# Roundings and a normalisation moved from VectorE to ScalarE in the last two attentions of a transformer stack

## The reference

```
x = x + tanh(g_xattn[2]) * L2_xattn(layernorm(x), ctx)     # 8 heads of 64, context of 64 tokens
x = x + tanh(g_ffn[2])   * L2_ffn(layernorm(x))
x = x + tanh(g_xattn[3]) * L3_xattn(layernorm(x), ctx)     # the same shapes
x = x + tanh(g_ffn[3])   * L3_ffn(layernorm(x))

def act_quant(x):                                          # in L2_ffn
    scale = 127.0 / clip(max(abs(x), axis=-1, keepdims=True), 1e-5, None)
    return clip(round(x * scale), -128.0, 127.0) / scale
h = square(relu(bitlinear(x, w_gate))) * bitlinear(x, w_up)   # 128 -> 512, ternary weights
y = bitlinear(h, w_down)                                   # bitlinear = act_quant(x) @ weight_quant(w).T
# L3_ffn: r = relu(x @ W.T), y = (r * r) @ W2.T
```

## Time and profile before

| what | us |
|---|---|
| median of 3 runs (1627.86 to 1633.79) | 1629.6 |
| the profiled execution | 1627.99 |
| its span | 1626.2 |
| the part with decoder's steps 11 to 41 | 246.08 |
| the 148.76 us behind it (second attention with the last feed-forward) | 148.76 |

### The profile page before, as it was taken

The page is one execution under the profiler, slowest core; times in us unless marked ns, Lnnn a source line. Parts: engine busy times, 40 slices in busy tenths (PEclk is TensorE's granted clock), DMA queues, the critical chain, the costliest instruction groups (busy, mean ns, idle before and its releaser), DMA issues.

```text
span 1626.2 us, 51062 instructions
## 1 busy us (share of the span) xinstructions
PE 1457.0 (90%) x18081; PEld 1101.7 (68%) x18081; DVE 1192.4 (73%) x4951; ACT 876.6 (54%) x1729; POOL 605.4 (37%) x1180
## 2 busy tenths in 40 slices
PE   6999999998999679898879779998998888899998
PEld 5888888875666345454476546666777677778886
DVE  6777777766777799999946844434889989866664
ACT  6665666554554455555303245554566666655553
POOL 4555545540000666666226411102333333334331
PEclk9999999998999587878659979997999999999999
DMA  8000000005300000000020010000000000000000
GB/s 194 2 0 0 0 0 0 0 1 117 76 0 3 12 0 0 0 0 0 1 64 0 0 34 0 0 0 2 2 2 1 0 1 2 2 2 14 6 14 21
DMA packets 41754, 23.37 MB, mean 14 GB/s; under 512 B 23325, under 2 KB 39162, under 8 KB 41530
## 3 DMA queue, kind: packets, MB, share of 16 engines
q1 hardware_dynamic: 41658, 22.07, 5.9%
HBM read 17.87 MB, written 4.19 MB: 14 GB/s over the span
## 4 chain that ended last, share of the span: by engine, by line
PE 60%; DVE 25%; issue 8%; ACT 3%; POOL 2%; DVEq 1%; DMA 0%; SPq 0%; POOLq 0%; ACTq 0%
PE ps L681 7%; PE ps L690 7%; DVE arena L1354 5%; DVE arena L1348 4%; PE ps L310 3%; PE ps L352 3%; PE ps L303 3%; PE ps L332 3%; PE ps L2058 2%; PE ps L2045 2%; PE ps L343 2%; PE ps L2132 2%; PE ps L2051 2%; PE ps L323 2%; PE ps L2101 2%
## 5 line engine op out<-in xcount | busy, mean ns | idle before, releaser
L681 PE MATMUL ps<-xnT,arena 128*128 128x512 f32 x256 | 134.8, 619 | 0.0
L574 POOL TENSOR_TENSOR ln_veps<-ln_mv,eps 128x4 f32<-128x4 f32 x40 | 10.7, 268 | 268.5 <-DVE ln_mv L568 268.5
L2557 POOL TENSOR_TENSOR arena<-arena 128x512 f32<-128x512 f32 x64 | 67.8, 1059 | 111.5 <-DVE arena L2481 111.5
L1810 DVE TENSOR_SCALAR_CACHE_REDUCE thr_hits<-thr_abs,thr_candidate 128x512 bf16<-128x512 f32 (+1 forms) x248 | 101.9, 477 | 0.0
L1354 DVE MATCH_REPLACE8 arena<-arena 128x64 f32<-128x64 f32 x512 | 101.7, 208 | 0.1
L830 DVE SCALAR_TENSOR_TENSOR x_res<-ps,arena,x_res 128x128 f32 (+1 forms) x256 | 72.0, 344 | 31.1 <-PE ps L690 28.5
L530 POOL TENSOR_TENSOR arena<-arena 128x1024 f32<-128x1024 f32 x32 | 61.4, 1918 | 54.1 <-DVE arena L484 54.1
L469 DVE TENSOR_REDUCE arena<-ps 128x16 f32<-128x1024 f32 x32 | 39.2, 1224 | 57.7 <-PE ps L323 57.7
L1348 DVE MAX8 arena<-arena 128x8 f32<-128x64 f32 x512 | 76.1, 210 | 6.6 <-POOL arena L1235 5.4
L690 PEld LDWEIGHTS ps<-arena 128*128 128x128 f32 x512 | 63.6, 191 | 25.4 <-issue 17.2
L1620 PE MATMUL ps<-ident,arena 128*64 128x128 f32 x256 | 43.1, 323 | 37.6 <-DVE arena L1406 37.6
(11 more groups left out here) (405 smaller groups left out, 4252.4 us busy)
## 6 DMA issues: line engine op xcount, KB each, us to landing
toeplitz<-ssm_toeplitz_scratch SPq DMA_DIRECT2D x2, 2048.0 KB, 18.0
ssm_toeplitz_scratch<-ssm_padded_kernel SPq DMA_DIRECT2D x1, 2048.0 KB, 12.9
out<-x_res SPq DMA_DIRECT2D x8, 256.0 KB, 2.3
arena<-ctx SPq DMA_DIRECT2D x2, 768.0 KB, 5.7
arena<-L_ffn_W SPq DMA_DIRECT2D x2, 512.0 KB
arena<-L_xattn_Wo SPq DMA_DIRECT2D x3, 256.0 KB, 8.8
arena<-L_xattn_Wq SPq DMA_DIRECT2D x1, 512.0 KB, 5.9
x_res<-x SPq DMA_DIRECT2D x1, 512.0 KB, 7.2
```

The costliest lines, as they stand in the source:

```text
L681: nc.tensor.matmul(ps[:, u % 3, :], w1[:, x, c * P:(c + 1) * P], xnT, start=True, stop=True).then_inc(h_full.sem, 1)
L1810: ins = V.tensor_scalar(self.hits[:, j, at:at + n], self.abs[:, at:at + n], self.cand[:, c:c + 1].bitcast(F32), 0.0, ALU.is_ge, ALU.add, a ...
L2557: G_.tensor_tensor(probs, probs, rc[:, s, :].unsqueeze(2).to_broadcast([P, heads, CTX]), ALU.mult).then_inc(s_prob.sem, 1)
```

## The change

1. The rounding of h (L2382) leaves VectorE. ScalarE does it, as an activation Identity with the scale of each partition and ROUND as bias, right behind its copy of head outputs.
2. The square (L2290) moves on ScalarE from behind the copy of probabilities to right behind the relu.
3. The normalising of four tiles (L2347) goes to ScalarE, behind its copy of keys, for both feed-forwards. For it GpSimd makes a bias: minus the mean times the reciprocal root, two more operations of 128x4 a round.
4. The rounding of the four tiles (L2367) goes to ScalarE, behind its copy of keys, one step after. VectorE's clip (L2371) moves to the next step, ahead of the clip of h.
5. The transpose of xn goes to PSUM bank 1 (columns 256 to 383) instead of bank 4, and no longer waits for the subtraction of the maximum.

```diff
@@ turn_xn, copy_xn @@
-        T_.transpose(ps[:, 4, 256:256 + P], xn[:, s, :], k.ident[:]).then_inc(xt_full.sem, 1)
+        T_.transpose(ps[:, 1, 256:256 + P], xn[:, s, :], k.ident[:]).then_inc(xt_full.sem, 1)
@@ pe_step @@
         if ahead(r, 1):
-            e.wait_ge(s_sub.sem, s_sub.at(t + 1))
             turn_xn(e, t + 1, o)
@@ act_step @@
             copy_heads(e, t)
+        if downs(r):
+            e.wait_ge(a_recip.sem, a_recip.at(t - F2))
+            e.wait_ge(hq_done.sem, hq_done.at(t - F2 - 1))
+            S.activation(hq[:], h[:], ACT.Identity, bias=magic[:, 0:1], scale=sh[:, 0:1]).then_inc(hr_done.sem, 1)
...
             S.activation(rl[:], ps[:, 6, :], ACT.Relu, scale=cgt[:, j:j + 1]).then_inc(r_done.sem, 1)
+            e.wait_ge(r_done.sem, r_done.at(t - F2 + 1))
+            e.wait_ge(h_done.sem, h_done.at(t - F2))
+            S.activation(r2[:], rl[:], ACT.Square).then_inc(r2_done.sem, 1)
...
-        if gates(r):
-            e.wait_ge(r_done.sem, r_done.at(t - F2 + 1))
-            e.wait_ge(h_done.sem, h_done.at(t - F2))
-            S.activation(r2[:], rl[:], ACT.Square).then_inc(r2_done.sem, 1)
         if ahead(r, 1):
             copy_queries(e, t + 1)
             copy_keys(e, t + 1)
+        if norms(r, 1):
+            e.wait_ge(n_shift.sem, n_shift.at(b))
+            if r >= F3 + 2:
+                e.wait_ge(x3_full.sem, x3_full.at(b - 9))
+            for j in range(GT):
+                last = S.activation(k.xn[:, 0, j, :], k.x[:, tile_at(t, r, j, 7), :], ACT.Identity, bias=n_bias[:, j:j + 1], scale=k.rstd[:, 0, j:j + 1])
+            last.then_inc(n_out.sem, 1)
+        if norms(r, 2) and r < LN3:
+            g = b - 2
+            e.wait_ge(q_step.sem, q_step.at(4 * g + 3))
+            for j in range(GT):
+                last = S.activation(qf[:, j, :], k.xn[:, 0, j, :], ACT.Identity, bias=magic[:, 0:1], scale=sc[:, j:j + 1])
+            last.then_inc(q_step.sem, 1)
@@ quantize, and dve_step behind the subtraction of the maximum @@
-        e.wait_ge(q_step.sem, q_step.at(n + 3))
-        for j in range(GT):
-            last = V.tensor_scalar(qf[:, j, :], k.xn[:, 0, j, :], sc[:, j:j + 1], ROUND, ALU.mult, ALU.add)
-        last.then_inc(q_step.sem, 1)
-        e.wait_ge(q_step.sem, q_step.at(n + 4))
+
+    def clip_q(e, g):
+        e.wait_ge(q_step.sem, q_step.at(4 * g + 4))
         e.wait_ge(qt_full.sem, qt_full.at(g))
         V.tensor_scalar(qb[:], qf[:], -ROUND, 127.0, ALU.add, ALU.min).then_inc(q_done.sem, 1)
...
+        if turns_q(r):
+            clip_q(e, b - 2)
         if downs(r):
             clip_h(e, t)
@@ scale_h @@
-        e.wait_ge(a_recip.sem, a_recip.at(n))
-        V.tensor_scalar(hq[:], h[:], sh[:, 0:1], ROUND, ALU.mult, ALU.add).then_inc(hr_done.sem, 1)
@@ pool_step, behind the reciprocal root of four tiles @@
+            G_.tensor_tensor(n_mean[:], k.mv[:, 0, :, 0], k.rstd[:, 0, :], ALU.mult).then_inc(n_mr.sem, 1)
...
+            G_.tensor_tensor(n_bias[:], n_zero[:], n_mean[:], ALU.subtract).then_inc(n_shift.sem, 1)
```

More of the change, by code:

```diff
@@ L1940, in decoder @@
     p_full, p_laid, y_full, x_done = sem("probsT_full", STEPS), sem("probsT_laid", STEPS), sem("y_full", STEPS), sem("x_added", STEPS)
-    n_stats, n_mv, n_ve, n_rs, n_out = (sem("group_" + n, NLN) for n in ("stats", "mv", "veps", "rstd", "normed"))
+    n_stats, n_mv, n_ve, n_rs, n_mr, n_shift, n_out = (sem("group_" + n, NLN) for n in ("stats", "mv", "veps", "rstd", "mean_scaled", "shift", "normed"))
     w2_in, w2_sum, w2_tot, w2_step, w2_tern = sem("f2_w_loaded", None), sem("f2_w_sums", 1), sem("f2_w_totals", 1), sem("f2_w_step", 7), sem("f2_w_ternary", 1)
@@ L1953, in decoder @@
     h3_full, r3_done, h3_laid = (sem("f3_" + n, IC * GROUPS) for n in ("h_full", "relu", "squared"))
-    out_done = k.sem("out_stored")
+    out_done, zeroed = k.sem("out_stored"), sem("zeroed", 1)
     cv = Carve(k.arena)
@@ L1970, in decoder @@
     am, sc, cgt, cut = (cv.f32(GT) for _ in range(4))
+    n_zero, n_mean, n_bias = (cv.f32(GT) for _ in range(3))
     qf, qb, qT = cv.f32(GT, D), cv.bf16(GT, D), cv.bf16(GT * P)
@@ L1973, in decoder @@
     hb, hT = cv.bf16(HID), cv.bf16(HID)
-    ah, sh, yc = cv.f32(1), cv.f32(1), cv.f32(1)
+    ah, sh, yc, magic = cv.f32(1), cv.f32(1), cv.f32(1), cv.f32(1)
     wf, wp, tf, tp = cv.f32(IC, D), cv.f32(HID), cv.f32(IC, D), cv.f32(HID)
@@ L2222, in copy_xn @@
         e.wait_ge(xt_full.sem, xt_full.at(t + 1))
-        S.copy(xnT[:, s * P:(s + 1) * P], ps[:, 4, 256:256 + P]).then_inc(xt_laid.sem, 1)
+        S.copy(xnT[:, s * P:(s + 1) * P], ps[:, 1, 256:256 + P]).then_inc(xt_laid.sem, 1)
     def copy_queries(e, t):
@@ L2340, in group_norm @@
             last.then_inc(n_mv.sem, 1)
[L2341 to L2345, removed]
-            for j in range(GT):
-                last = V.tensor_scalar(k.xn[:, 0, j, :], k.x[:, tile_at(t, r, j, 7), :], k.mv[:, 0, j, 0:1], k.rstd[:, 0, j:j + 1],
-                                       ALU.subtract, ALU.mult)
-            last.then_inc(n_out.sem, 1)
         if norms(r, 2) and r < LN3:
@@ L2396, in dve_weights @@
                 V.tensor_reduce(sums[:, i:i + 1], wraw[:, i, :], AX.X, ALU.add, apply_absolute_value=True)
+            V.memset(magic[:], ROUND)
             V.tensor_copy(identb[:], k.ident[:]).then_inc(w2_sum.sem, 1)
@@ L2481, in dve_step @@
             V.reciprocal(rc[:, s, :], sm[:, s, :]).then_inc(s_rec.sem, 1)
-        if norms(r, 1) or norms(r, 2):
+        if norms(r, 2):
             group_norm(e, t, r, b)
@@ L2543, in pool_step @@
             G_.tensor_tensor(k.rstd[:, 0, :], k.veps[:, 0, :], k.half[:], ALU.pow).then_inc(n_rs.sem, 1)
+            e.wait_ge(n_rs.sem, n_rs.at(b))
+            if r > LN2:
+                e.wait_ge(n_out.sem, n_out.at(b - 1))
+            e.nop(nofuse=True)
+            G_.tensor_tensor(n_mean[:], k.mv[:, 0, :, 0], k.rstd[:, 0, :], ALU.mult).then_inc(n_mr.sem, 1)
+            e.wait_ge(n_mr.sem, n_mr.at(b))
+            e.nop(nofuse=True)
+            if r == LN2:
+                e.wait_ge(zeroed.sem, zeroed.at(1))
+            G_.tensor_tensor(n_bias[:], n_zero[:], n_mean[:], ALU.subtract).then_inc(n_shift.sem, 1)
         if ahead(r, 2):
@@ L2560, in pool @@
         e.wait_ge(before.sem, before.end)
+        G_.memset(n_zero[:], 0.0).then_inc(zeroed.sem, 1)
         for t in range(2):
```

## The result

| | before | changed |
|---|---|---|
| median of 6 runs, us | 1631.46 (1627.86 to 1633.92) | 1614.21 (1611.26 to 1616.83) |
| ratio to before | | 0.9898 (0.9881 to 0.9915) |
| span of the profiled run, us | 1626.2 | 1614.3 |

The kernel is 1.0% faster, 17 us; the forecast was 1609 in 1594 to 1620. The spans differ by only 11.9. Up to the first subtraction of the decoder, in code that the change doesn't touch, the changed profile took 1115.38 and that of before 1110.67 us.

What follows compares the result with a forecast made beforehand. It took a circle of VectorE and ScalarE, with TensorE waiting, to bound the fused stretch. Gains of 19.9 + 1.0 + 0.4 less 0.6 made 20.7 us, from 1627.99 to 1607.3; with 1.6 for the median, 1609, range 1594 to 1620.

Steps and rivals of the forecast that it cites:

- VectorE's relief: Fused stretch: VectorE loses 4.6 of its 28.28 us a round and no longer sets the round.
- ScalarE's prices: Moved work on ScalarE: rounding of h 0.83 us, small activations 0.53; its round goes from 20.84 to some 27.
- The stalls on top of the floor: Five TensorE delays a round, 0.6, 0.5, 0.55, 0.4 and 0.15 us, added to 26.6 to give 28.8.
- The projection behind the two batches: Output projection held behind ScalarE's normalising (0.5 us) and rounding of four tiles (0.55) in each round.
- Transposes of h: TensorE's transposes of h come late: 0.4 us in the fourth step, 0.15 in the first.
- Keys: Keys wait for the copy of transposed h, delayed by the earlier square: 0.15 us a step, 0.6 a round.
- The multiplier: Fused stretch, steps 11 to 41: 2.57 us gained a round, times 7.75 rounds, 19.9 us.
- last stretch: The 148.76 us behind the fused stretch: 0.2 us gained a round from moving the normalising, five rounds, 1.0 us.
- my own case: The main forecast, with a round of 28.8 us and a time of 1600 to 1619; chance 0.68.
- TensorE alone is left: Rival: small activations cheap and ScalarE's queue has slack, round 26.6 to 27.2 us, time about 1594; chance 0.17.
- the work only changes place: Rival: each ScalarE batch holds TensorE its whole 1.6 us, round 30.95, time about 1626; chance 0.09.
- ScalarE as the slower engine: Rival: small activations at 0.9 us each make a round 32.8 us, time 1640; chance 0.06.

Runs made afterwards that it cites:

- turn_only: The kernel before with only the transpose of xn in bank 1 and no wait for the subtraction; ratio to before 0.9983.
- h_only: The kernel before with only the rounding of h moved to ScalarE; ratio to before 0.9902.
- own_bank: The changed kernel with transposed h and tiles in otherwise unused halves of banks 4 and 3, so keys need not wait; ratio to before 0.9831, median 1604.64 us.
- norm_back: The changed kernel with the normalising of four tiles back on VectorE, without GpSimd's two operations; ratio to before 0.9895.
- norm_only: The kernel before with only the normalising of four tiles on ScalarE, with GpSimd's operations for it; ratio to before 0.9984.
- wait_back: The changed kernel with the transpose of xn back in bank 4, waiting for the subtraction; ratio to before 0.9888.
- h_back: The changed kernel with the rounding of h back on VectorE; ratio to before 0.9946.
- round_back: The changed kernel with the rounding of four tiles back on VectorE, its clip still one step later; ratio to before 0.9910.
- own_square_norm: The changed kernel with separate banks for transposed h and tiles, the square behind the copy of probabilities, normalising on VectorE; ratio to before 0.9837.

## Why the prediction was right, and where it was off

**The range and the sign** held: 1614.2 in 1594 to 1620. The gain was 17 us instead of 20.7, a fifth less.

**The bound before** was read rightly as a circle of VectorE and ScalarE on which TensorE waits. turn_only shows that the wait at the subtraction was a sign of it and no cause.

**VectorE's relief.** The sum took 4.6 us of VectorE's work as one thing ("It no longer sets the round"). The runs part it: of the three, the rounding of h alone gives 1.55 us a round and 13 of the 16 us; the normalising 0 to 0.3 a round; the rounding of four tiles 0.3, in the company of the rest. What was missing in my reading is where each stands. The rounding of h is on the circle in all four steps. The relief was also smaller than 4.6: VectorE went from 28.28 to 24.90, 3.4. The four roundings of h took 1.6 off (28.28 to 26.68 in h_only), since the next instruction starts before they end; I had taken their whole length, 1.9.

**ScalarE's prices** were right: 0.83 forecast and 0.814 measured for the rounding of h, 0.53 and 0.485 for the small ones, "some 27" and 26.86 for the round.

**The stalls on top of the floor** are what was mis-sized. Forecast 28.8 a round, measured 29.20. The projection behind the two batches: 1.05 forecast, 1.2 measured. Transposes of h: 0.55 forecast (0.4 in the fourth step, 0.15 in the first); the row reads 1.4 in all four, but the kernel before has 1.1 of the same wait within what I took as the floor, so 0.3 came on top:

```profile
PEld ps L2154 <- DVE x_res L2470: 1.1, 4, 0.3
```

Keys: "I take 0.15 a step (bounds 0 and 0.25), 0.6 in a round", measured 1.7. That is the term that failed. It left out that the copy of the four tiles stands ahead of the keys too, in the step where they are 0.66 late. It took the square at 0.55 of the queue, as if it overlapped the relu; but it reads what the relu writes and starts when that has ended (0.73 behind its start, the copy of before 0.58), so the copy of transposed h starts 1.27 us behind the relu instead of 0.58, 0.69 later. And it took off a lateness of TensorE that did not come: in the first three steps of the round its queries begin 0.52 to 0.61 us behind the relu, 0.57 before. own_bank measures what the keys' wait is worth when removed: 1.1 us a round, half a microsecond more than forecast, and that is about what the forecast missed. The three waits added to 26.6 are 29.8, more than the 29.20: they are waits of weight loads, and ahead of the keys' matmuls the idle time is only 0.9.

**The multiplier.** 2.17 us a round by 7.75 is 16.8; the stretch gave 15.95, of which 1.3 is the clock. The other rounds at full clock gave 1.84 to 2.17, and at the end of the stretch it was lost: step 40 took 9.23 us against 8.49 before. norm_back has 8.47 there, so what costs is ScalarE's batch of the normalising ahead of that step.

**Around it**: last stretch 1.4 gained (1.0 forecast). The cause that I gave, the normalising taken from VectorE, is half of it at most: with the wait in place it gives 0.7 (148.0 in norm_only and in wait_back, 148.8 before), but the removed wait gives all of the 1.4 (147.4 in turn_only and in norm_back), and then the normalising adds nothing. Tail 0.5 lost (0.6); first steps 0.3 lost instead of 0.4 gained.

**The width.** The bounds given for three of the five stalls have half widths of 0.98 us together, and 1.4 if the second batch has those of the first, not the 1.2 of the forecast; with 1.4 the range of my own case would have been 2 us wider on each side.

**The rivals.** That TensorE alone is left did not come: 29.20 against 27. That the work only changes place is nearly true of the normalising alone (0 to 0.3 us a round). As to ScalarE as the slower engine: the Trainium skill ("ScalarE: Activation LUTs", Rules for kernel authors) gives adding and multiplying to VectorE. For the length of the roundings the trace agrees: ScalarE needs 814 ns for the rounding of h against 486, and 484 for one of the four tiles against 282. (So it was wrong to say that the rule holds only for the four tiles; and the 521 ns of a normalising were a little less than the forecast 0.53, though ScalarE's then measured 485.) For the time of the step the trace does not bear it out: h_back, which follows the rule, is 0.85 us a round slower, and round_back 0.3.

Left open: why own_square_norm's second step costs more than its third gives back; what the rounding of four tiles and part 5 are worth with the late square; and why the clock was lower in some rounds of before and of norm_only.

## What to carry to other kernels

When work moves between engines, ask not how full each engine is but whether the instruction stands on the circle that sets the step: 0.41 us on it counted in each of four steps, 1.8 us beside it gave 0 to 0.3 a round. Undo the parts of a mixed change one by one: here one part carried most of it, one was a cost hidden under the gain (the early square, 0.8 us a round), and its cause (a PSUM bank shared by a copied and a waiting tile) led to the faster version. Compare parts in both companies, too: three of them looked worth little beside the early square and 9.7 us without it. A wait at which an engine stands long may be worth nothing if the same late instruction is waited for again a little further on.

## What the runs showed of the hardware that I had not expected

VectorE's clip of the four tiles reads 427 ns before and 700 in the changed kernel, the same instruction at another place, right behind the subtraction and beside GpSimd's addition to x:

```profile
1268.23 0.46 POOL L2570 TENSOR_TENSOR x_res<-x_res,toeplitz 128x128 f32 x1
1268.27 0.70 DVE L2376 TENSOR_SCALAR arena<-arena 128x512 bf16<-128x512 f32 x1
```

The clip of h, of the same shape, shows that the order decides. In the kernel before, it reads 0.42 without the addition beside it and 0.53 where the addition has started first and ends 0.24 us into it:

```profile
1246.59 0.42 DVE L2390 TENSOR_SCALAR arena<-arena 128x512 bf16<-128x512 f32 x1
...
1269.74 0.45 POOL L2554 TENSOR_TENSOR x_res<-x_res,toeplitz 128x128 f32 x1
1269.95 0.53 DVE L2390 TENSOR_SCALAR arena<-arena 128x512 bf16<-128x512 f32 x1
```

In the changed kernel the clip sometimes starts first. Then it keeps its length and the addition takes 0.63 instead of 0.46:

```profile
1224.76 0.43 DVE L2393 TENSOR_SCALAR arena<-arena 128x512 bf16<-128x512 f32 x1
...
1224.87 0.63 POOL L2570 TENSOR_TENSOR x_res<-x_res,toeplitz 128x128 f32 x1
```

Between 1215 and 1280 us of both traces every clip goes by this pattern: it is 0.1 us or more longer where the addition started first and had 0.2 us or more still to run, and within 0.02 of its 0.42 otherwise. No run takes the addition away, so this is read from the traces and not tested.
